# Aligned records read by the pair, and gathers in fours that wait for their landing, in a four-layer graph network on one core

## What is computed

```python
h = jnp.maximum(_layernorm(x, axis=-1), 0.0)
xs, xv = (s @ W_s)[edge_src], (v @ W_v)[edge_src]      # one table row per edge
w = act(edge_features @ W_fc1) @ W_fc2                 # layers 0, 1 and 3
products = w * xs, w * xv, with the edge's four attributes
agg = jax.ops.segment_sum(products, edge_dst, num_segments=N)
x = x + linear(agg) + skip
```

## Time and profile before

| | us |
|---|---|
| median of 3 runs | 8062.31 |
| least, most | 8038.93, 8091.24 |
| span of the profiled execution | 8211.3 |
| busy in it: PE, PEld | 5036.2, 4316.2 |
| busy in it: DVE, ACT, POOL | 3476.8, 3472.5, 4006.1 |
| POOL, gathers of layers 1 to 3 (L899, 2346) | 2225.6 |
| POOL, gathers of layer 0 (L875, 880) | 832.5 |

### The profile page before, as it was taken

One profiled execution on the slowest core, in us unless ns is written; L12 is line 12 of the kernel. 1 busy time (PEld: TensorE's weight loads), 2 busy tenths in 40 slices (PEclk: granted clock), 3 DMA queues, 4 the chain that ended last, 5 costly groups with the idle time before them and its releaser, 6 DMA issues. The chain is left out here.

```text
span 8211.3 us, 118595 instructions
## 1 busy us (share of the span) xinstructions
PE 5036.2 (61%) x24426; PEld 4316.2 (53%) x24427; DVE 3476.8 (42%) x11481; ACT 3472.5 (42%) x14717; POOL 4006.1 (49%) x4467
## 2 busy tenths in 40 slices
PE   5254611057777777867777777644444666766777
PEld 3132301046666666756666666533333666666666
DVE  5253500035555555634444444422222544444455
ACT  0000000024444433445555555566666645555554
POOL 6535255545444545444444444566655444444444
PEclk7576755578888888978888888755555788888888
DMA  8212122223222223121111111122222121121211
GB/s 274 94 38 52 30 56 55 53 57 63 60 59 63 61 59 63 35 56 49 48 47 48 48 46 45 50 64 63 64 63 64 46 51 50 49 50 46 51 50 39
DMA packets 643944, 484.23 MB, mean 59 GB/s; under 512 B 437482, under 2 KB 551593, under 8 KB 643707
## 3 DMA queue, kind: packets, MB, share of 16 engines
q0 software_dynamic: 181776, 292.84, 14.1%
q1 hardware_dynamic: 379563, 149.21, 7.5%
q10 hardware_dynamic: 82496, 40.92, 1.7%
HBM read 400.40 MB, written 96.88 MB: 61 GB/s over the span
## 5 line engine op out<-in xcount | busy, mean ns | idle before, releaser
L899 POOL DMA_INDIRECT gath<-table,small x2346 | 2225.6, 949 | 2171.4 <-DVE work L1498 1248.8
L1070 ACT ACTIVATE sel<-acc,rows 128x32 f32<-128x32 f32 x10560 | 2347.7, 310 | 453.1 <-issue 430.2
L1481 DVE TENSOR_TENSOR acc<-acc,bank 128x160 f32 (+1 forms) x3520 | 1209.7, 344 | 2361.6 <-remote 792.3
L1903 PE MATMUL bank<-work,sel 128*128 128x160 f32 (+1 forms) x5280 | 1517.2, 373 | 643.9 <-DVE acc L1481 582.7
L1877 PE MATMUL bank<-w,work 128*128 128x224 f32 (+2 forms) x5280 | 1319.9, 378 | 677.9 <-ACT work L1053 261.6
L1877 PEld LDWEIGHTS bank<-w,work 128*128 128x128 f32 (+1 forms) x5280 | 1022.0, 216 | 812.4 <-issue 487.8
L1903 PEld LDWEIGHTS bank<-work,sel 128*128 128x128 f32 x5280 | 1041.5, 221 | 745.4 <-DVE acc L1481 653.8
L1905 PE MATMUL bank<-work,sel 128*128 128x160 f32 x5280 | 1304.6, 333 | 0.0
L875 POOL DMA_INDIRECT gath<-table,rows x880 | 832.5, 946 | 891.1 <-DVE work L1515 337.6
L752 POOL DMA_INDIRECT rows_a<-acc x782 | 750.3, 960 | 840.1 <-ACT acc L989 607.2
L1905 PEld LDWEIGHTS bank<-work,sel 128*128 128x128 f32 x5280 | 1058.6, 220 | 60.5
(11 more groups left out here) (296 smaller groups left out, 3706.8 us busy)
## 6 DMA issues: line engine op xcount, KB each, us to landing
rows<-rows_b SPq DMA_DIRECT2D x330, 128.0 KB
gath<-table,small POOLq DMA_INDIRECT x2346
rows_a<-acc ACTq DMA_DIRECT2D x1, 30360.0 KB, 102.8
rows<-rows_a SPq DMA_DIRECT2D x110, 256.0 KB
acc<-in_rows_a SPq DMA_DIRECT2D x34, 793.5 KB
gath<-table,rows POOLq DMA_INDIRECT x880
acc<-in_rows_b SPq DMA_DIRECT2D x34, 368.0 KB
rows_a<-acc POOLq DMA_INDIRECT x782
```

The lines of the kernel that those rows point to most:

```text
L899: pool.indirect_dma_start(gath_all[:, u, :], None, table_dram[n][:, :], bass.IndirectOffsetOnAxis(ap=index_r[q][:, u:u + 1], axis=0)).then ...
L1070: i = act.activation(sel[q][:, t, at:at + BIN], hot, ACT.Copy, scale=e[:, k:k + 1])
L1481: dve.tensor_tensor(sums, sums, bank(6 + b, P, 256 * h, 256 * h + L.width), ALU.add).then_inc(S["fl"].sem, 1)
L1903: pe.matmul(out, sel[qv][:, t, 96:224], work[:, a + NF:a + NF + L.width], start=True, stop=False, skip_group_check=True)
```

## The change

The record grows to 32 words (128 bytes) and is laid out by the pair: four times [2 bins, 2 places], then the two counts. DVE loads the two counts at a group's start and each pair's four words (two in layer 2) at the pair; PE in layer 2 loads 18 words. SP fills the records by 14 small DMAs instead of 6. The weights turned at the start of layer 2 move from `acc` to `side`, to make room. POOL in layer 0 waits after each fourth gather until it and the three before have landed; in layers 1 and 3 it does so too, and reports `arrived` at once. Layer 2 keeps its gathers.

```diff
-RECORD = 2 * GT + 2
+RECORD = 32
+PAIR_WORDS = 4
+NEED_AT = PAIR_WORDS * PAIRS
...
-        turned_w = acc[:, fold_at:fold_at + 8 * 192].rearrange("p (i c r) -> p i c r", i=8, c=2)
-        onehot_at = fold_at + 8 * 192
+        turned_w = side[:, 0:8 * 192].rearrange("p (i c r) -> p i c r", i=8, c=2)
+        onehot_at = BINS * LAYERS[1].width + TCOLS * P
...
-        NODE_LOADS = 9
+        NODE_LOADS = 5 + 3 * PAIRS
...
-                sp.dma_start(records[:, 0, 0:2 * LAG_FL], bins[:, 0:2 * LAG_FL]).then_inc(s_nodes_of, 16)
-                sp.dma_start(records[:, 0, 2 * LAG_FL:GT], bins[:, 0:at]).then_inc(s_nodes_of, 16)
-                sp.dma_start(records[:, 1:, 0:GT], bins[:, at:at + GROUPS * GT].rearrange("a (g r) -> a g r", r=GT)).then_inc(s_nodes_of, 16)
-                sp.dma_start(records[:, :, GT:2 * GT], guide_dram[1:2, 0:(GROUPS + 1) * GT].rearrange("a (g r) -> a g r", r=GT)).then_inc(s_nodes_of, 16)
+                for u in range(PAIRS):
+                    a, k = 2 * u, PAIR_WORDS * u
+                    first = bins[:, a:a + 2] if u < LAG_FL else bins[:, a - 2 * LAG_FL:a - 2 * LAG_FL + 2]
+                    sp.dma_start(records[:, 0, k:k + 2], first).then_inc(s_nodes_of, 16)
+                    sp.dma_start(records[:, 1:, k:k + 2], later[:, :, a:a + 2]).then_inc(s_nodes_of, 16)
+                    sp.dma_start(records[:, :, k + 2:k + 4], slots[:, :, a:a + 2]).then_inc(s_nodes_of, 16)
...
@@ body (layer 0), POOL
+                        if u % HALF == HALF - 1:
+                            wait(pool, S[f"ga{q}{u // HALF}"], half * (16 * HALF) + 16 * HALF)
+                            pool.sem_inc(s_apart["pool"], 1)
@@ columns, POOL
-                        if v == HALF - 2 and (h or not is_static(r) or r):
+                        if n != 2 and v == HALF - 1:
+                            wait(pool, S[f"gc{h}"], r * (16 * HALF) + 16 * HALF)
+                            pool.sem_inc(S["arrived"].sem, 1)
+                        if n == 2 and v == HALF - 2 and (h or not is_static(r) or r):
                             wait(pool, S[f"gc{(h - 1) % 4}"], (r + (1 if h else 0)) * (16 * HALF))
                             pool.sem_inc(S["arrived"].sem, 1)
@@ edges, DVE
-                        _, record = nc.values_load_multi_w_load_instructions(
-                            guide[0:1, bass.ds(g * RECORD, RECORD if L.mlp and L.compact else GT)], engines=(DVE,), min_val=0,
-                            max_val=(RING_COLS - 1) * NF, ...)
+                    elif L.mlp:
+                        _, need = nc.values_load_multi_w_load_instructions(
+                            guide[0:1, bass.ds(g * RECORD + NEED_AT, 2)], engines=(DVE,), min_val=0, max_val=HALVES, ...)
                     for u in range(PAIRS):
                         i = g * PAIRS + u
+                        if n:
+                            _, four = nc.values_load_multi_w_load_instructions(
+                                guide[0:1, bass.ds(g * RECORD + PAIR_WORDS * u, PAIR_WORDS if L.mlp else 2)], engines=(DVE,), ...)
@@ edges, PE in layer 2
-                            guide[0:1, bass.ds(g * RECORD + GT, GT + 2)], engines=(TENSOR,), ...)
+                            guide[0:1, bass.ds(g * RECORD, NEED_AT + 2)], engines=(TENSOR,), ...)
```

More of the change, by code:

```diff
@@ L267, in gnn_program @@
         guide_at = onehot_at + 2 * GT * BIN
+        assert guide_at % 16 == 0
         guide = acc[0:1, guide_at:guide_at + (GROUPS + 1) * RECORD].bitcast(I32)
@@ L650, in _ @@
             with nc.allow_non_contiguous_dma(reason="a record per group"):
-                sp.dma_start(records[:, 0, 0:2 * LAG_FL], bins[:, 0:2 * LAG_FL]).then_inc(s_nodes_of, 16)
-                sp.dma_start(records[:, 0, 2 * LAG_FL:GT], bins[:, 0:at]).then_inc(s_nodes_of, 16)
-                sp.dma_start(records[:, 1:, 0:GT], bins[:, at:at + GROUPS * GT].rearrange("a (g r) -> a g r", r=GT)).then_inc(s_nodes_of, 16)
-                sp.dma_start(records[:, :, GT:2 * GT], guide_dram[1:2, 0:(GROUPS + 1) * GT].rearrange("a (g r) -> a g r", r=GT)).then_inc(s_nodes_of, 16)
+                slots = guide_dram[1:2, 0:(GROUPS + 1) * GT].rearrange("a (g r) -> a g r", r=GT)
+                later = bins[:, at:at + GROUPS * GT].rearrange("a (g r) -> a g r", r=GT)
+                for u in range(PAIRS):
[4 more added lines that the diff above has]
+                    sp.dma_start(records[:, :, k + 2:k + 4], slots[:, :, a:a + 2]).then_inc(s_nodes_of, 16)
                 for h in range(2):
-                    sp.dma_start(records[:, :, 2 * GT + h],
+                    sp.dma_start(records[:, :, NEED_AT + h],
                                  guide_dram[2:3, 0:(GROUPS + 1) * GT].rearrange("a (g r) -> a g r", r=GT)[:, :, HALF * h + HALF - 1]).then_inc(s_nodes_of, 16)
@@ L906, in columns @@
                         h = (count - 1) // HALF
-                        if (count - 1) % HALF < HALF - 2:
+                        if n == 2 and (count - 1) % HALF < HALF - 2:
                             wait(pool, S[f"gc{(h - 1) % 4}"], (r + (1 if h else 0)) * (16 * HALF))
@@ L1526, in edges @@
                             skip_runtime_bounds_check_because="counts of at most BINS bins, less one")
-                    else:
-                        _, record = nc.values_load_multi_w_load_instructions(
-                            guide[0:1, bass.ds(g * RECORD, RECORD if L.mlp and L.compact else GT)], engines=(DVE,), min_val=0,
-                            max_val=(RING_COLS - 1) * NF, skip_runtime_bounds_check_because="bins, places in the ring, counts of half groups")
-                        bins = [nc.s_assert_within(v, 0, BINS - 1, skip_runtime_bounds_check_because="bins") for v in record[0:GT]]
-                        slots, need = record[GT:2 * GT], record[2 * GT:]
+                    elif L.mlp:
+                        _, need = nc.values_load_multi_w_load_instructions(
+                            guide[0:1, bass.ds(g * RECORD + NEED_AT, 2)], engines=(DVE,), min_val=0, max_val=HALVES,
+                            skip_runtime_bounds_check_because="counts of half groups")
                     for u in range(PAIRS):
                         i = g * PAIRS + u
+                        if n:
+                            _, four = nc.values_load_multi_w_load_instructions(
+                                guide[0:1, bass.ds(g * RECORD + PAIR_WORDS * u, PAIR_WORDS if L.mlp else 2)], engines=(DVE,), min_val=0,
+                                max_val=(RING_COLS - 1) * NF, skip_runtime_bounds_check_because="bins, places in the ring")
+                            bins[2 * u:2 * u + 2] = [nc.s_assert_within(v, 0, BINS - 1, skip_runtime_bounds_check_because="bins")
+                                                     for v in four[0:2]]
+                            slots[2 * u:2 * u + 2] = four[2:]
                         if within(i - L.lag_fl, TILES // 2):
@@ L1912, in edges @@
                         _, record = nc.values_load_multi_w_load_instructions(
-                            guide[0:1, bass.ds(g * RECORD + GT, GT + 2)], engines=(TENSOR,), min_val=0, max_val=(RING_COLS - 1) * NF,
+                            guide[0:1, bass.ds(g * RECORD, NEED_AT + 2)], engines=(TENSOR,), min_val=0, max_val=(RING_COLS - 1) * NF,
                             skip_runtime_bounds_check_because="places in the ring, counts of half groups")
-                        slots, need = record[0:GT], record[GT:]
+                        slots, need = [record[PAIR_WORDS * (t // 2) + 2 + t % 2] for t in range(GT)], record[NEED_AT:]
                     for u in range(PAIRS):
```

3 lines of the change are left out of this document (1 added, 2 removed).

## The result

The changed kernel takes 7873.12 us (7869.38 to 7885.23, four runs), the kernel before 8071.07 beside it (8038.93 to 8091.24): a ratio of 0.977, interval 0.9748 to 0.9794. The gain is 198 us; 736 were forecast. The profiled execution is 7883.7 us against 8211.3, a ratio of 0.960: by the profiles the gain is 328 us. The difference lies in the kernel before, whose profiled execution is longer than any of its four runs, while that of the changed kernel is one of its runs.

A forecast was written before the change was run, and what follows sets the result against it. No engine is full; waits bound the kernel, from PE semaphores held during gathers and from register loads. Layers 0 to 3 give -250 - 284 - 42 - 176, plus 2 between layers: -750, scaled to -736, 7325 us; range 7070 to 7720.

The forecast's parts named there:

- A half costs POOL 3 x 1.25 + 2.2 + 0.3 to go on = 6.25 us: Layers 0, 1, 3: waiting for landing after each fourth gather makes POOL's half 6.25 us where it was 5.0.
- It is hidden where POOL has slack: POOL's added 765 us stay off the path: floors of 12.7 us a group (layer 0) and 11.4 (layers 1, 3).
- the scale: Whole kernel: profiled span 1.8% above the runs' median, so the -750 us sum is scaled by 0.982 to -736.
- Holds: PE's semaphores held back while POOL's gathers stream; runs cut to four pay 2.1 us each, layer 0 gains 250 us.
- The loads: DVE's register loads, layers 1 and 3: aligned records, two words 0.37 us, four 0.32; on the path 1.17 against 2.82.
- Half is taken: Layers 1 and 3: of the three later four-word loads, 0.96 us together, half (0.48) counts as on the path.
- Layer 2: Gathers kept; PE's 18 aligned words and DVE's four two-word loads save 0.4 us a group, 42 us; bounds -100 and +45.
- Rival 2: Nothing but POOL binds: layers 0, 1 and 3 at POOL's floors of 12.7, 11.5, 11.5; 7045 us; chance 0.12.
- Rival 1: Semaphores are held by gathers per time, not run length; fours stall like eights, only loads gain; 7665 us; chance 0.17.
- rival 5: Records not aligned after all: 8-byte pieces, 0.9 a pair, some +1.5 us a group; 7700 us; chance 0.04 with others.
- rival 4: Splitting the load costs a floor per load, 0.55 us each of five in layers 1 and 3; 7550 us; chance 0.08.
- Rival 3: Semaphore delays stay and the landing wait lies in the product-release-gather loop; slower, 8420 us; chance 0.09.

The follow-up runs named there:

- The control: The changed kernel plus a bitwise and, leaving the value alone, on each loaded count that is waited against; 7933.26 us against 8245.54 before, 0.961.
- Three of four: Changed kernel with masks, but POOL goes on when three of each half's four gathers have landed; 7449.41 us, 0.905 of the kernel before.
- records only: Changed kernel with masks, without the landing waits, so only new records and loads; 0.998 of the kernel before, and 0.969 on a chip without late semaphores.
- masked kernels: Follow-up kernels whose loaded, waited-against counts are and-ed with 255 or 4095, values unchanged; the kernel before with masks alone took 1.009 on a chip without late semaphores.

## Why the prediction was wrong

**The step that failed** is a term of the sum: "A half costs POOL 3 x 1.25 + 2.2 + 0.3 to go on = 6.25 us". The 2.2 was right (2.24). The 0.3 is the gap between two gathers of a run; after a wait it is 1.32, of which some 0.5 until DVE, which waits for the same landing, starts, and 0.8 more until POOL's gather does. The trace of before had the second part, in a row just behind the earlier trace rows that the prediction does not use:

```profile
2626.54 0.81 DVE L1515 TENSOR_TENSOR work<-bank,gath 128x288 f32<-128x288 f32 x2
...
2628.17 0.94 POOL L875 DMA_INDIRECT gath<-table,rows  x1 [5.51 <-DVE work L1515]
```

The product ends at 2627.35 and the gather that it releases starts 0.82 later. With the whole turn in the sum the floors are 14.6 and 13.3 instead of 12.7 and 11.4, above what was forecast for each layer. So the sentence "It is hidden where POOL has slack" fails with it: there was no slack left.

How much it explains, on the profiled spans: 750 us were forecast and 328 came. The new floors leave 74 + 185 + 132 = 391 of the 710 us forecast for the three layers, so this term is 319 of the 422 missing; layer 2 is 50 (below), and most of the rest is that the layers run 0.1 to 0.3 us a group above the floors.

**A second term, the scale.** "The span is 1.8% above the median of the runs ... so I scale by 0.982" took the profiled execution of the kernel before to stand for its runs. The changed kernel's is only 0.2% above its median, so by the runs the gain is another 130 us less, 198 instead of 328. The control (0.961) says that the profiles' 0.960 is what a second chip gives; why the first kernel's runs were faster than its profiled execution stays open.

Three of four is a check of the sum, though of another kernel: there a half does cost 6.2, the layers take 12.5, 12.6 and 12.4 against the forecast 13.0, 12.4 and 12.9, and the ratio is 0.905 against a forecast 7325 / 8062 = 0.909. That both agree so well is in part luck, since layer 1 keeps most of its late updates there.

**Holds** were read rightly: they follow runs of gathers, and in layer 0 the pauses end them (455 late updates to 21). But their price of 2.1 us a run of four no longer counted, since POOL was later, and so stays untested. That a set of runs can have none was nowhere in the forecast.

**The loads** are 0.53 us for two words (forecast 0.37) and 0.34 for four (forecast 0.32); 1.57 to 1.60 aligned for 18 words, as forecast. With holds they are nearly off the path: records only took 0.998. "Half is taken" was a guess about what hides them; with holds nearly all was hidden, without holds they gave 1.0 us a group.

**Layer 2** gained nothing (+8 us, forecast -42); its four loads of two words take 0.53 each, 2.1 a group instead of the 1.6 forecast. The stretch from the last compare of layer 0 to the first of layer 1 went from 138.0 to 146.0 us, +8 for +2; with records only it is 139.5, so the records cost what was forecast and the rest comes with the waits.

**The rivals.** Rival 2 had the mechanism, all three layers at POOL's pace, with the same wrong floor, so its 7045 was further off. Rival 1 falls by the late updates, rival 5 by the load lengths (its own sum gives 7650 and not 7700). Of rival 4 the lengths came for two words (0.53) and not for four. Rival 3 did not come true here, but on the chip without holds on which the changed kernel ran the landing waits are a pure cost (1.195 of before). So the rule of the Trainium skill, "DMA: Bandwidth & Descriptors", section "Rules for kernel authors", to wait for a DMA late, was broken at a gain of 2 to 4% where semaphores are held, and at a loss of 19% where they are not. That it gains is not shown to be the landing's doing: a pause without any look at it ends the holds as well (22 late updates).

## What to carry to other kernels

Cost a wait by the whole turn: from the last packet to the start of the waiting engine's next work, read at a place where that engine already waits, not from its back-to-back spacing. When a wait is added to an engine that is half idle, work out its new floor a group and compare it with each layer's time; 1 us a half that the sum lacked put layer 0 1.9 us a group above its forecast. Do not scale a profiled span to the runs by one kernel's ratio. A stall that no instruction explains may belong to the chip or the hour and not to the program: profile the kernel more than once, on other chips, before tuning against it.

## What the runs showed of the hardware

- PE's semaphore updates can come late while POOL issues gathers, and in other sets of runs of the same kernel none does. In three sets the kernel before took 8071, 8246 and 8233 us, in the four later ones 5898 to 5912. Instructions are as long in both (a gather 0.95, DVE's 128x256 product 0.42). Late in layer 0 of the kernel before: 455 of 1418 in the one kind, 0 of 1492 in the other. What makes the difference is open.
- Holds show ahead of layer 0 too, where POOL issues 782 indirect writes: 167 of 1147 updates late in the control, none of 1212 in the same kernel without holds, and layer 0 starts at 1713.7 us against 1112.4.
- How short a pause still helps where there are holds stays open below 1.5 us: the runs for it fell on chips without. So does whether the landing matters at all or only the pause.
- A register load's time goes by alignment: 18 words take 1.57 us when records are aligned, and 4.06 or 1.57 in turn when they are not. Two words took 0.53 us and four 0.34, so it does not simply grow with the words.
- The way from the last packet of a gather: 0.45 us to DVE's product that waits for it, 1.32 to the next gather of a POOL that waits for it; from the end of a product of DVE to the gather that it releases 0.8.
- In layer 2 with holds the masked kernels with new records took 11.4 to 11.5 us a group, those with old records 11.17 and 11.31, the unmasked ones 11.14 and 11.21; on chips without holds all that keep its gathers take 8.9. That was not followed up.
